# Fourth unit of attention: two transposes behind the values, half a feed-forward layer behind the second projection

## What is computed

```
x = x + 0.5 * moe(norm(x))          # top 2 of 8 experts, hidden 512
y = norm(x);  x = x + block(y)      # block(y) = attention and feed-forward, below
x = x + 0.5 * moe(norm(x))

def block(y):                       # per sequence of 256 tokens, 16 heads of 64
    z = norm(y) * g1 + b1
    Q, K, V = phi(z @ Wq), phi(z @ Wk), z @ Wv         # phi = elu + 1
    num = causal (Q K^T) V;  den = causal sum of Q K^T
    a = y + (num / den) @ Wo
    h = norm(a) * g2 + b2
    return a + gelu(h @ Wf1) @ Wf2
```

## Time and profile before

| | us |
|---|---|
| median of 3 runs | 2107.47 (2105.28 to 2109.17) |
| the profiled execution | 2108.45 |
| its span | 2105.6 |
| TensorE busy | 1702.6 (81%) |
| VectorE busy | 1502.8 (71%) |
| ScalarE busy | 1064.3 (51%) |
| GpSimd busy | 945.1 (45%) |

### The profile page before, as it was taken

The page is one execution under the profiler, slowest core; times in us unless marked ns, Lnnn a source line. Parts: engine busy times, 40 slices in busy tenths (PEclk is TensorE's granted clock), DMA queues, the critical chain, the costliest instruction groups (busy, mean ns, idle before and its releaser), DMA issues. The chain is left out here.

```text
span 2105.6 us, 36420 instructions
## 1 busy us (share of the span) xinstructions
PE 1702.6 (81%) x12531; PEld 1380.8 (66%) x12531; DVE 1502.8 (71%) x4213; ACT 1064.3 (51%) x1929; POOL 945.1 (45%) x1071
## 2 busy tenths in 40 slices
PE   3342599996599999999999999999999825999960
PEld 2232477775478877878787877777878624777750
DVE  6664477775688888888888888888887534777753
ACT  1210466664455555555555555555555314666640
POOL 5777155556423243444344434443443150555560
PEclk9999999998799999999999999999999857999995
DMA  5442476763100000100010001010100005666638
GB/s 165 156 156 86 178 246 231 249 217 116 18 9 11 7 18 10 22 16 18 10 22 17 18 10 21 17 18 10 22 16 8 5 31 200 230 222 225 228 116 240
DMA packets 89312, 190.31 MB, mean 90 GB/s; under 512 B 15869, under 2 KB 54442, under 8 KB 78122
## 3 DMA queue, kind: packets, MB, share of 16 engines
q1 hardware_dynamic: 50986, 133.29, 18.6%
q0 software_dynamic: 27392, 46.18, 8.1%
q10 hardware_dynamic: 10752, 8.52, 1.2%
HBM read 131.08 MB, written 56.85 MB: 89 GB/s over the span
## 5 line engine op out<-in xcount | busy, mean ns | idle before, releaser
L511 POOL DMA_INDIRECT expert_rows<-f_rows_out,f_dest x312 | 311.4, 998 | 316.9 <-DVE f_rows_out L729 244.0
L1288 POOL TENSOR_TENSOR at_sc<-at_sc 128x512 f32<-128x512 f32 x128 | 169.1, 1321 | 428.7 <-DVE at_sc L1406 428.4
L436 ACT ACTIVATE f_hid<-f_up_ps,f_w 128x512 f32<-128x512 f32 x312 | 214.6, 688 | 171.0 <-PE f_up_ps L346 148.6
L1398 DVE SCALAR_TENSOR_TENSOR at_qk<-at_exps,at_relus 128x512 f32<-128x512 f32 x256 | 177.4, 693 | 131.6 <-ACT at_relus L1197 131.1
L1406 DVE TENSOR_TENSOR at_sc<-at_s_ps,at_mask 128x384 f32<-128x384 f32 x512 | 251.7, 549 | 1.1 <-PE at_s_ps L1021 1.1
L706 DVE TENSOR_TENSOR f_hid_lo<-f_hid,f_hid_hi 128x512 fp32r<-128x512 f32 x312 | 208.2, 689 | 14.4
L1261 ACT ACTIVATE raw<-at_num_ps 128x512 f32<-128x512 f32 x128 | 76.3, 596 | 222.1 <-PE at_num_ps L1058 213.8
L1018 PE MATMUL at_s_ps<-at_qk 64*128 64x256 f32 x1024 | 171.0, 411 | 6.4 <-issue 5.6
L1196 ACT ACTIVATE at_exps<-at_proj_ps 128x512 f32<-128x512 f32 x253 | 152.3, 602 | 34.0 <-PE at_proj_ps L996 27.1
L1053 PE MATMUL at_num_ps<-at_sc,at_vals 128*64 128x256 f32 x1024 | 162.6, 396 | 6.2 <-DVE at_den L1558 6.1
L702 DVE CAST f_hid_hi<-f_hid 128x512 fp32r<-128x512 f32 x156 | 66.7, 427 | 133.9 <-issue 122.0
(11 more groups left out here) (292 smaller groups left out, 4611.4 us busy)
## 6 DMA issues: line engine op xcount, KB each, us to landing
f_w<-split_weights SPq DMA_DIRECT2D x78, 1028.0 KB
f_got<-sent_rows SPq DMA_DIRECT2D x78, 264.0 KB
split_weights<-f_split SPq DMA_DIRECT2D x8, 1024.0 KB
x<-expert_rows POOLq DMA_DIRECT2D x64, 128.0 KB, 3.2
f_w<-expert_rows SPq DMA_DIRECT2D x32, 256.0 KB, 4.0
expert_rows<-f_rows_out,f_dest POOLq DMA_INDIRECT x312
sent_rows<-f_pads ACTq DMA_DIRECT2D x16, 264.0 KB, 2.9
x<-in_L_attn_x SPq DMA_DIRECT2D x16, 256.0 KB, 5.8
```

The source lines that it names most:

```text
L436: A(hid[:, c, :], up_ps[n % 4][:, :], ACT.Silu, bias=w[:, i % RING_W, 4 * HID + c:4 * HID + c + 1].bitcast(FP32)).then_inc(s_silu, 1)
L511: g.indirect_dma_start(out=k.back[:, :], out_offset=bass.IndirectOffsetOnAxis(dest[:, i % RING_DEST, q:q + 1], 0), in_=rows_out[:, i % RIN ...
L1288: g.tensor_tensor(sc[:, n % RING_SC, :, 3, :], sc[:, n % RING_SC, :, 1, :], sc[:, n % RING_SC, :, 2, :], ALU.add).then_inc(s_sum, 1)
L1398: stt(full, exps[:, p % 2, :], 1.0, relus[:, p % 2, :], ALU.min, ALU.add).then_inc(s_phi, 1)
```

## The change

In the fourth unit, TensorE does the value products first and then the transposes of the two norms, with their waits; `ffn_up(0)` with its waits goes behind the second q/k projection. ScalarE takes the numerators' copy before the affine passes. Nothing else differs.

```diff
--- before.py
+++ after.py
@@ -1108,15 +1108,6 @@
                     if u == 0 and has_down(s):
                         pe.wait_ge(s_gelu, 2 * (s - 2) + 1)
                         ffn_up(2)
-                    if u == 3 and (has_z(s) or has_rest(s)):
-                        if has_rest(s):
-                            pe.wait_ge(s_an, s)
-                        else:
-                            pe.wait_ge(s_z, s + 3)
-                            pe.wait_ge(s_hT_hi, 2)
-                        if has_hidden(s):
-                            pe.wait_ge(s_hidden, 2 * (s - 2))
-                        transpose_slot(has_z(s), has_rest(s))
                     if u == 1 and has_down(s):
                         pe.wait_ge(s_gelu, 2 * (s - 2) + 2)
                         if has_rest(s):
@@ -1137,6 +1128,15 @@
                     if u == 2 and has_rest(s):
                         pe.wait_ge(s_o, 4 * (s - 1) + 4)
                         output_product((s - 1) % 2)
+                    if u == 3 and (has_z(s) or has_rest(s)):
+                        if has_rest(s):
+                            pe.wait_ge(s_an, s)
+                        else:
+                            pe.wait_ge(s_z, s + 3)
+                            pe.wait_ge(s_hT_hi, 2)
+                        if has_hidden(s):
+                            pe.wait_ge(s_hidden, 2 * (s - 2))
+                        transpose_slot(has_z(s), has_rest(s))
                     v = ("v", s + (u + 2) // UNITS, ((u + 2) // 2) % 2, u % 2)
                     if v in number and s < NB:
                         project(v)
@@ -1155,11 +1155,6 @@
                         broadcast(2)
                     if ("qk", g + 3, 0) in number:
                         project(("qk", g + 3, 0))
-                    if u == 3 and has_rest(s):
-                        pe.wait_ge(s_h2_lo, s)
-                        if has_z(s):
-                            pe.wait_ge(s_hT_hi, s + 3)
-                        ffn_up(0)
                     if u == 2 and has_hidden(s):
                         if has_rest(s):
                             pe.wait_ge(s_a, s)
@@ -1171,6 +1166,11 @@
                         router_hidden()
                     if ("qk", g + 3, 1) in number:
                         project(("qk", g + 3, 1))
+                    if u == 3 and has_rest(s):
+                        pe.wait_ge(s_h2_lo, s)
+                        if has_z(s):
+                            pe.wait_ge(s_hT_hi, s + 3)
+                        ffn_up(0)
                     if u == 0 and has_rest(s):
                         pe.wait_ge(s_o, 4 * (s - 1) + 1)
                         broadcast(1)
@@ -1249,6 +1249,9 @@
                     if u == 0 and has_down(s):
                         gelu(s, "up2", 2)
                         A(warm[:, 0:1], k.minus_half[:, 0:1], ACT.Exp)
+                    if s < NB:
+                        act.wait_ge(s_num, g + 1)
+                        A(num[s % 2][:, u, :], num_ps[:, :], ACT.Copy).then_inc(s_num_out, 1)
                     if u == 3 and (has_z(s) or has_rest(s)):
                         act.wait_ge(s_slot, fill(s, "z_an"))
                         if has_rest(s):
@@ -1256,9 +1259,6 @@
                             affine(h2_hi[:, :], ROW_G2, slot_ps[:, BT:2 * BT], s_h2_hi)
                         if has_z(s):
                             z_out(s + 2)
-                    if s < NB:
-                        act.wait_ge(s_num, g + 1)
-                        A(num[s % 2][:, u, :], num_ps[:, :], ACT.Copy).then_inc(s_num_out, 1)
                     if s < NB or u == 1:
                         for what in projected(g):
                             if u == 2 and has_hidden(s) and what == ("qk", g + 3, 1):
```

## The result

| | before | after |
|---|---|---|
| median of 6 runs, us | 2106.38 (2092.78 to 2109.17) | 2130.62 (2125.59 to 2133.57) |
| the profiled execution, us | 2108.45 | 2125.59 |
| its span, us | 2105.6 | 2123.1 |

The change makes the kernel slower: ratio 1.0118, 95% interval 1.0091 to 1.0144, about 24 us (19 to 30 by the interval). The range of the prediction holds it; the point forecast of 2119.0 has the right side and half the size. Three more runs of before are in this median, and with them before reaches down to 2092.78. The profiled execution of the change is the fastest of its six, so the two profiled executions are only 17 us apart.

A forecast was written before the change was run, and what follows sets the result against it. Attention was taken to last as long as TensorE's work plus its stops. Odd units +1.6, blocks 1 to 4 +3.5 and even units with sends +6.4 gave +11.5 us on the median 2107.47: 2119.0 us, range 2109.0 to 2138.0.

The forecast's parts named there:

- The removed wait: TensorE's transposes wait for VectorE's `an`, 18.2 us in 31 stops; behind the value products it is covered, worth 16.
- The new stop: Second q/k projection of each fourth unit waits 1.06 us for ScalarE's values' copy; +1.6 odd units, +3.5 blocks 1 to 4.
- The half behind the projection: The 0.71 us feed-forward half, now after the second projection, covers nothing; its own inputs are ready, so it doesn't wait.
- The even units with sends: 13 even-block fourth units with POOL's sends: transposes' signal on time, only the values' projection told late; +6.4 us.
- rival 1: In even units with sends the late signal hits the transposes: +24.9 in place of 6.4, total 2131 to 2137; chance 0.22.
- Rival 2: TensorE's clock also falls behind longer projection stops, half of 3.4 us lost in 13 units, adding 22: about 2158; chance 0.08.
- The same chain: Fourth unit: transposes, four affine passes, values' copy, second projection in sequence; 6.17 us from scores to next scores, nothing told late.

The follow-up runs named there:

- e3: Against the changed kernel, ScalarE's copy of the projected values moved between the affine passes for h2 and those for hT; 2076.61 us, before 2071.24.
- e2: Against the kernel before, only the feed-forward half moved behind the second q/k projection, transposes and numerators' copy left in place; 2078.24 us, before 2071.24.
- e1: Against the changed kernel, the feed-forward half put back between the two q/k projections; 2091.84 us, before 2071.24.
- r2_after_again: The changed kernel once more, no edit, beside the kernel before on one chip; 2086.76 us, before 2070.57, ratio 1.0075.
- e8: Against the changed kernel, ScalarE's values' copy between the affine passes and VectorE's last expert-choice steps behind unit 3; 2080.78 us, before 2071.34.
- r3: The changed kernel without an edit, a single run for one look on the other chip; 2089.25 us, before 2071.34.

## Why the prediction came out as it did

**The removed wait.** Right for blocks 1 to 30, where no wait for `an` is left. The prediction took the longest of the 31 stops, 1.95 in block 31, for one of a block without values and left it standing; the earlier trace rows show value products right behind it, and it fell to 0.5. So 17.7 us of waits went, not 16.

**The new stop.** Right in place, kind and size. 1.06 was worked out and 1.11 stands in the trace with the row's own count of idle time (the projection starts 4.55 behind the scores' end, 4.54 was worked out); odd units and blocks 1 to 4 take 6.13 to 6.17, with 6.17 said. e3 moved only the copy it hangs on, and the stop fell to 0.19.

**The half behind the projection.** Right that its own inputs are in time there and that its cover was worth little: e2 has 0.23 us a unit; and e1 shows that between the projections it would itself be late.

**The even units with sends: the step that failed.** The forecast took the transposes' signal as told on time ("I take on time, and keep the other as a rival") and gave these units +6.4. The signal was late. In 12 of the 13 units the affine passes began at E + 3.44 to 3.51, within 0.1 of where rival 1 put them (1205.18 - 1201.67 = 3.51). The term of +6.4 was +22.3, with -5.9 at the denominators, stops that rival 1 let go by up to 5.9. Rival 1's sum, 1.6 + 3.5 + 24.9 - 5.9, gives 24.1; on the median 2131.6, and 2130.62 was measured. It had 0.22, the forecast 0.47. That its total fits to 1 us is partly luck: its +24.9 stands against 20 us of late signals and 2.3 of clock in the trace, and the two traces are 17.5 apart, not 24. Late or on time was called near even. The trace shows a delay that begins by E + 1.5: the value products' signal, due then, is told at E + 2.7, and the transposes', due at E + 2.04, at E + 3.5. Before had a sign of it: in blocks 6, 16 and 24 the affine passes already began 0.4 later behind the scores than in the other even blocks. The argument against, that the scores' signals aren't late, rested on no one waiting for them and showed nothing either way. The longer of the two delays of before, to E + 4.2, came in one unit only, that of block 30, which is why rival 1's +24.9 was too much.

**The clock.** Rival 2 came in 2 of the 13 units, at 1.1 and 1.2 us, not 1.7 in all 13: stops of 2.5 us were followed by a stretch at 0.50 twice and left it at 1.00 eleven times. The Trainium skill, TensorE: Matmul & The Clock Gate, section on psum-queue depth-cycling, tells of a kernel whose clock swung with brief, frequent idling between groups of matmuls. Carried over to this kernel, as rival 2 did, the clock should have swung with a stop of 1.1 us in every fourth unit. In the changed kernel it fell twice between 700 and 1600 us, both times behind a stop of 2.5, and in r2_after_again, with stops of 1.1 in 29 units, not once in that stretch. The measurement decides: these stops cost no clock.

**What it missed.** That the late signals belong to the chip, or to what it was doing then, and not to the program. On the two chips of the experiments the loss was 16.2 us and, in a single run, 17.9. The same chain gives both numbers, from 5.24 as the even unit's time before.

**What stays open.** What makes a signal late. In both first traces it happens in the 13 fourth units with sends and in some of the first units behind them, and in no other fourth unit; but no run here took the sends away where there are late signals. Nor is it settled how much of the 35 us between the chips they make. The change's two traces, the first and r2_after_again, are 37.2 us apart in span. 22.9 of these lie between the fourth units of blocks 1 and 30, 19.2 of them in the even units; 17.3 lie ahead of the scores' end of block 1, most of it in the first layer; behind block 30 the first is 3.0 us shorter. Late signals stand in the first layer of before too, again beside sends of GpSimd (TensorE's router product ends at 46.68, VectorE, 1.87 us idle, starts on it at 48.88), so they may have a part in the 17.3; that isn't shown. TensorE's wait for fetched rows (`f_got`) ahead of block 1 is 40.5 us in the change's first trace against 29.5 in r2_after_again.

## What to carry to other kernels

A wait that is taken away by moving its consumer is paid again where the consumer's result is due: follow the result through the next engine's queue, in its order, to the bank or buffer that sets the next start, and compare the two arrival times there before counting the wait as won. Here the better cure stood at the producer: three small steps moved behind the late norm gave 7.8 us, with TensorE's order untouched. And a unit's time should be read on the kind of chip that it is judged on; a delay that only some blocks show may not be the program's.

## What the runs showed that was not expected

- The same program has signals of TensorE told about 2 us late in the first traces (the value products end at 1132.52, the copy behind them starts at 1134.42; the denominators end at 1139.79, VectorE starts on them at 1142.01), and none over 0.3 us late in attention in the traces from the two chips of the experiments.
- VectorE's 128x256 subtraction took 0.42 us beside a send of GpSimd, 1.27 beside its 128x512 sum and 1.91 where it began in a send with the sum behind. In blocks 1 to 30 TensorE waited for the slow ones in e1, e3 and e8 and, at block 30, in r2 and r3.
- Stops of 2.5 us, once in each second block, were followed by a fall of TensorE's granted clock to 0.50 in 2 of 13 cases, for 3.4 us each.
